# Two joined pair sums a unit, maxima turned in the row scores' ring, inverse sums half a unit later, and an identity in PSUM

## What is computed

```python
xn = _layernorm(x)
# attention: 32 heads of 32 channels, 8 key/value heads
q, k, v = (bitnet_linear(xn, w, s) for w, s in ((q_weight, q_scale), (k_weight, k_scale), (v_weight, v_scale)))
scores = einsum('bhqd,bhkd->bhqk', q, k) / sqrt(32)
attn = softmax(scores)
att = bitnet_linear(einsum('bhqk,bhkd->bhqd', attn, v), o_weight, o_scale)
# FFN: 1024 -> 3584 -> 1024
gate, up = silu(xn @ deq(gate_w)), xn @ deq(up_w)
out = x + att + (gate * up) @ deq(down_w)
```

## Time and profile before

| | us |
|---|---|
| median of 3 runs (lowest, highest) | 2314.91 (2314.68, 2315.96) |
| the profiled execution | 2313.24 |
| its span in the profile | 2311.2 |
| TensorE busy | 2259.1 (98%) |
| VectorE busy | 1808.2 (78%) |
| ScalarE busy | 1591.1 (69%) |
| GpSimd busy | 1036.6 (45%) |

### The profile page before, as it was taken

How to read it: one execution, slowest core, us unless ns; L and a number is a source line. 1 busy time by engine, 2 the same in 40 slices (tenths; PEclk the granted TensorE clock), 3 DMA queues, 4 the chain that set the end, 5 groups by cost and what they waited for, 6 DMA issues and landing times.

```text
span 2311.2 us, 44481 instructions
## 1 busy us (share of the span) xinstructions
PE 2259.1 (98%) x18195; PEld 1015.9 (44%) x18195; DVE 1808.2 (78%) x2305; ACT 1591.1 (69%) x2059; POOL 1036.6 (45%) x598
## 2 busy tenths in 40 slices
PE   6999999999999999999999999999999999999998
PEld 4444344444444444334444444444445444444444
DVE  8878888888888888856677777777777777777777
ACT  6774788888888888852466666666666666666664
POOL 0450689999999999930055553210003222221000
PEclk9999999999999999999999999999999999999999
DMA  5893444444444444433387884131114111114111
GB/s 188 170 205 97 112 92 102 104 94 109 100 107 94 101 106 96 113 97 110 119 107 94 95 97 64 37 119 37 37 64 146 37 37 43 48 39 183 37 37 73
DMA packets 187888, 216.38 MB, mean 94 GB/s; under 512 B 88402, under 2 KB 128210, under 8 KB 186662
## 3 DMA queue, kind: packets, MB, share of 16 engines
q1 hardware_dynamic: 114742, 151.67, 20.8%
q0 software_dynamic: 72944, 61.88, 20.0%
HBM read 164.28 MB, written 69.64 MB: 101 GB/s over the span
## 4 chain that ended last, share of the span: by engine, by line
PE 90%; DVE 5%; ACT 2%; issue 1%; SPq 1%; DMA 1%; DVEq 0%; ACTq 0%; POOL 0%
PE ps L1759 33%; PE ps L1775 17%; PE ps L1523 9%; PE ps L1576 9%; PE ps L1590 9%; PE ps L1728 5%; PE ps L1607 4%; PE ps L1548 3%; DVE zone L1184 1%; DVE sm L1049 1%; ACT zone L869 1%; DVE zone L1088 1%; PE ps L1791 0%; DVE zone L1294 0%; ACT zone L849 0%
## 5 line engine op out<-in xcount | busy, mean ns | idle before, releaser
L1759 PE MATMUL ps<-xT,zone 128*128 128x512 f16 x3584 | 774.2, 379 | 0.0
L1203 DVE TENSOR_REDUCE zone<-ps 128x1 f32<-128x512 f32 x1024 | 636.5, 681 | 102.7 <-PE ps L1523 98.5
L869 ACT ACTIVATE zone<-ps,sm 128x512 f32<-128x512 f32 x1024 | 623.9, 695 | 101.5 <-PE ps L1576 98.4
L690 POOL TENSOR_TENSOR xT<-zone 128x1024 f32<-128x1024 f32 x252 | 617.2, 2675 | 127.0 <-ACT zone L869 127.0
L1440 DVE TENSOR_SCALAR ps<-ps,zone_c 128x1024 f32<-128x1024 f32 x392 | 506.8, 1293 | 162.4 <-PE ps L1759 160.3
L992 ACT ACTIVATE ps<-ps,zone_c 128x1024 f32<-128x1024 f32 x392 | 426.6, 1088 | 248.3 <-PE ps L1759 248.3
L1759 PEld LDWEIGHTS ps<-xT,zone 128*128 128x128 f16 x3584 | 350.6, 98 | 422.5 <-DVE zone L1444 0.3
L1576 PE MATMUL ps<-zone 98*32 98x512 f16 x4096 | 412.9, 381 | 5.9 <-ACT zone L869 4.2
L1523 PE MATMUL ps<-zone 96*32 96x512 f16 (+1 forms) x3946 | 411.2, 380 | 3.6 <-DVE zone L1203 3.6
L1775 PE MATMUL ps<-zone 128*128 128x512 f16 x1792 | 387.1, 379 | 0.0
L1451 DVE TENSOR_SCALAR ps<-ps,zone_c 128x1024 f32<-128x1024 f32 x216 | 279.3, 1293 | 93.0 <-PE ps L1775 92.8
(11 more groups left out here) (141 smaller groups left out, 1438.7 us busy)
## 6 DMA issues: line engine op xcount, KB each, us to landing
zone<-dequantised SPq DMA_DIRECT2D x84, 512.0 KB, 3.7
xT<-xT POOLq DMA_DIRECT2D x31, 1024.0 KB, 8.7
dequantised<-zero_points SPq DMA_DIRECT2D x56, 256.0 KB, 4.0
zone<-zone SPq DMA_DIRECT2D x384, 32.0 KB, 1.9
zone<-_attn_hidden_states_dram SPq DMA_DIRECT2D x16, 512.0 KB, 6.3
zone<-inverse_sums SPq DMA_DIRECT2D x128, 64.0 KB, 2.6
attention<-zone SPq DMA_DIRECT2D x32, 256.0 KB, 2.2
xT<-attention SPq DMA_DIRECT2D x4, 2048.0 KB, 12.1
```

The costliest lines, as they stand in the source:

```text
L690: nc.gpsimd.tensor_tensor(pairs[:, j, hp, :], prob[:, prob_slot(e), :], prob[:, prob_slot(e + 2), :], add).then_inc(s["sum_ok"], 1)
L869: A(prob[:, prob_slot(e), m % 2 * 512:(m % 2 + 1) * 512], ps[:, 3 + m % 3, :], ACT.Exp, scale=gam[:, 0:1]).then_inc(s["exp_ok"], 1)
L1203: V.tensor_reduce(mxs[:, u % 2, half, i % 16:i % 16 + 1], ps[:, (2 * i + half) % 3, :], AX, amax).then_inc(s["max_ok"], 1)
L1759: last = MM(ps[:, 4 * s2 + 2 * m + c, :], ring[:, buf, m * H + g * P:m * H + (g + 1) * P], xT[:, hf, part, g, c * 512:(c + 1) * 512], star ...
```

## The change

`joined_late` holds for units 0 to 29. There `join_late` adds pair sum 2 to pair sum 3 by a second adding DMA, so only j = 1 (k = 2) and j = 3 go through the ones, the latter at k = 12. The maxima are turned into a place of the row scores' ring: `row_place` leaves one out for them in each unit, and the row groups behind them wait accordingly. The steps behind the sums move: `evacuate_sums` to k = 13, `compact_sums` to k = 15, `invert` to k = 6 of the next unit, `store_inverse` to k = 7, `spread_inverse` to k = 13, `head_of` to k = 7, `divide` and `tail_of` to j = 0 and j = 1 of the unit after. `turn_maxima` also turns an identity into PSUM, and `common_maxima` reads it there. In the last turns, ScalarE and GpSimd do two blocks of four in the first two quarters, and stores take two blocks each.

```diff
+def joined_late(u):
+    return u < UNITS - 2
...
-    return 3 * u
+    return 2 * u if u < UNITS - 1 else 2 * u + 1
...
-    return ones_before(u) + (((None, 1, 0, 2) if joined(u) else (0, 1, 2, 3))[j])
+    return ones_before(u) + (((None, 0, None, 1) if joined_late(u) else (None, 1, 0, 2) if joined(u) else (0, 1, 2, 3))[j])
...
+def row_place(c):
+    return c + max(0, (c - 34) // 32)
+def maxima_place(u):
+    return 33 * u + 33 if u else None
...
                     load_v(u // 2 + 1)
-                if k == 7 and u:
+                if k == 7 and u >= 2:
+                    store_inverse(u - 2)
+                if k == (15 if u < UNITS - 1 else 7) and u:
...
                     load_m(u + 1)
-                if k == 5 and u >= 2:
+                if k == 13 and u >= 2:
...
                     load_k(u // 2 + 2)
-                if k == 15 and u:
+                if k == 15 and u == UNITS - 1:
...
-            def store_blocks(n):
-                for b in range(4):
-                    sp.wait_ge(s["turn_ok"], 8 + 4 * n + b + 1)
-                    sp.dma_start(rows_of(out, 1, n)[:, b, :], rows(1, n)[:, b, :]).then_inc(s["out_ok"], 16)
+            def store_turned(n):
+                sp.wait_ge(s["turn_ok"], 8 + 2 * n + 2)
+                sp.dma_start(rows_of(out, 1, n)[:, 0::2, :], rows(1, n)[:, 0::2, :]).then_inc(s["out_ok"], 16)
+            def store_mixed(n):
+                sp.wait_ge(s["mix_ok"], 8 + 2 * n + 2)
+                sp.dma_start(rows_of(out, 1, n)[:, 1::2, :], rows(1, n)[:, 1::2, :]).then_inc(s["out_ok"], 16)
+            def store_pair(n, a):
+                sp.wait_ge(s["turn_ok"], 12 + 4 * (n - 2) + 2 * a + 2)
+                sp.dma_start(rows_of(out, 1, n)[:, 2 * a:2 * a + 2, :], rows(1, n)[:, 2 * a:2 * a + 2, :]).then_inc(s["out_ok"], 16)
...
                 load_block(k)
-            for n in range(4):
-                store_blocks(n)
-            sp.wait_ge(s["out_ok"], 16 * (4 + 16))
+            store_turned(0)
+            store_turned(1)
+            store_pair(2, 0)
+            store_mixed(0)
+            store_pair(2, 1)
+            store_mixed(1)
+            store_pair(3, 0)
+            store_pair(3, 1)
+            sp.wait_ge(s["out_ok"], 16 * (4 + 8))
...
                     pool.wait_ge(s["quad_ok"], 16 * u)
+                elif j == 2 and joined_late(u - 1):
+                    pool.wait_ge(s["late_ok"], 16 * u)
...
+            def join_late(u):
+                pool.wait_ge(s["sum_ok"], duo_of(u, 3, 1) + 1)
+                nc.gpsimd.dma_start(pairs[:, 3, :, :], pairs[:, 2, :, :], accum_op=add, max_dma_last_dim=4096).then_inc(s["late_ok"], 16)
...
                         join_pairs(u)
-                    if u >= 2 and j == 1:
-                        divide(u - 2)
-                    if u >= 2 and j == 3:
-                        tail_of(u - 2)
-            for u in range(UNITS - 2, UNITS):
+                    if j == 3 and joined_late(u):
+                        join_late(u)
+                    if u >= 3 and j == 0:
+                        divide(u - 3)
+                    if u >= 3 and j == 1:
+                        tail_of(u - 3)
+            for u in range(UNITS - 3, UNITS):
...
-            def mix_rows(n):
-                pool.wait_ge(s[f"xr_in{n % 2}"], 16 * (n // 2 + 1))
+            def mix_rows(hf, n):
+                pool.wait_ge(s[f"xr_in{n % 2}"], 16 * (n // 2 + 1) if hf == 0 else 16 * 4)
                 for b in (1, 3):
-                    pool.wait_ge(s["half_ok"], 2 * n + (b + 1) // 2)
-                    nc.gpsimd.tensor_tensor(rows(0, n)[:, b, :], rows(0, n)[:, b, :], turned(n)[:, b // 2, :], add).then_inc(s["mix_ok"], 1)
+                    pool.wait_ge(s["half_ok"], 2 * (4 * hf + n) + (b + 1) // 2)
+                    nc.gpsimd.tensor_tensor(rows(hf, n)[:, b, :], rows(hf, n)[:, b, :], turned(n)[:, b // 2, :], add).then_inc(s["mix_ok"], 1)
...
                         n = 2 * TURNS.index((t + 1) // 2)
-                        mix_rows(n)
-                        mix_rows(n + 1)
+                        mix_rows(0, n)
+                        mix_rows(0, n + 1)
...
                         add_attention(hf, oh, s2)
+            mix_rows(1, 0)
+            mix_rows(1, 1)
...
                     evacuate_values(u - 1)
-                if k == 5 and u:
+                if k == 7 and u >= 3:
+                    head_of(u - 3)
+                if k == (13 if u < UNITS - 1 else 5) and u:
                     evacuate_sums(u - 1)
-                if k == 14 and u >= 2:
-                    head_of(u - 2)
...
                     evacuate_sums(UNITS - 1)
+                elif n == 2:
+                    head_of(UNITS - 3)
...
-            def act_turn(n, s2):
+            def act_turn(hf, n, s2):
                 th = n % 2
+                if hf == 1:
+                    act.wait_ge(s["second_pe"], 2 * HALF_VISITS)
                 for b in (1, 3):
-                    i = 4 * th + b
-                    act.wait_ge(s["turn_pe"], 4 * n + b + 1)
-                    if n >= 2:
-                        act.wait_ge(s["mix_ok"], 2 * (n - 2) + (b + 1) // 2)
+                    i = 8 * hf + 4 * th + b
+                    act.wait_ge(s["turn_pe"], 4 * (4 * hf + n) + b + 1)
+                    if hf or n >= 2:
+                        act.wait_ge(s["mix_ok"], 2 * (4 * hf + n - 2) + (b + 1) // 2)
...
                         for th in range(2):
-                            act_turn(2 * TURNS.index(j) + th, th)
+                            act_turn(0, 2 * TURNS.index(j) + th, th)
...
                             act_down(hf, oh, it, s2)
+            act_turn(1, 0, 0)
+            act_turn(1, 1, 1)
...
                     dve.wait_ge(s["s_pe"], 2 * i + half + 1)
-                    V.tensor_reduce(mxs[:, u % 2, half, i % 16:i % 16 + 1], ps[:, (2 * i + half) % 3, :], AX, amax).then_inc(s["max_ok"], 1)
+                    V.tensor_reduce(mxs[:, u % 2, half, i % 16:i % 16 + 1], ps[:, row_place(2 * i + half) % 3, :], AX, amax).then_inc(s["max_ok"], 1)
...
                 dve.wait_ge(s["m_pe"], u + 1)
-                m = ps[0:16, 7, 0:P]
+                m = ps[0:16, maxima_place(u) % 3 if u else 7, 0:P]
...
                 settle()
-                V.tensor_scalar(diag, id32[0:2 * IT, 0:2 * IT], cmt, None, mult).then_inc(s["dg_ok"], 1)
+                V.tensor_scalar(diag, ps[0:2 * IT, 0, P:P + 2 * IT], cmt, None, mult).then_inc(s["dg_ok"], 1)
...
                     common_maxima()
-                if k == 14 and u:
+                if k == 6 and u >= 2:
+                    invert(u - 2)
+                if k == 14 and u == UNITS - 1:
...
                 dve.wait_ge(s[f"xr_in{n % 2}"], 16 * (n // 2 + 1) if hf == 0 else 16 * 4)
-                for b in range(4) if hf else (0, 2):
+                for b in range(4) if hf == 1 and n >= 2 else (0, 2):
...
                 c = 2 * i + half
-                if c >= 3:
+                if c >= 66 and (c - 34) % 32 == 2:
+                    pe.wait_ge(s["mrow_ok"], (c - 34) // 32 + 1)
+                elif c >= 66 and (c - 34) % 32 < 2:
+                    pe.wait_ge(s["max_ok"], c - 1)
+                elif c >= 3:
...
                     c0 = i % 4 * P + a
-                    last = MM(ps[a:a + wide, c % 3, :], qst[u % 4][0:96, i % 16 // 4, c0:c0 + wide],
+                    last = MM(ps[a:a + wide, row_place(c) % 3, :], qst[u % 4][0:96, i % 16 // 4, c0:c0 + wide],
...
                 pe.wait_ge(s["top_ok"], u + 1)
-                if u >= 2:
-                    pe.wait_ge(s["evd_ok"], u - 1)
-                MM(ps[0:16, 7, 0:P], mtop, id32[:], start=True, stop=True).then_inc(s["m_pe"], 1)
+                if u:
+                    pe.wait_ge(s["max_ok"], 32 * u + 32)
+                MM(ps[0:16, maxima_place(u) % 3 if u else 7, 0:P], mtop, id32[:], start=True, stop=True).then_inc(s["m_pe"], 1)
...
             def pair_sums(u, j):
-                first, last_round = ((2, 3) if joined(u) else (0, 3))
+                first, last_round = (1 if joined_late(u) else 2 if joined(u) else 0), 3
...
                     pe.wait_ge(s["quad_ok"], 16 * (u + 1))
+                if j == 3 and joined_late(u):
+                    pe.wait_ge(s["late_ok"], 16 * (u + 1))
                 if j == first:
-                    pe.wait_ge(s["mrow_ok"], min(u + 2, UNITS))
...
                 pe.wait_ge(s["max_ok"], 2 * STEPS)
+                pe.wait_ge(s["mrow_ok"], UNITS)
...
                 pe.wait_ge(s["cmx_ok"], 1)
+                TR(ps[0:2 * IT, 0, P:P + 2 * IT], id32[0:2 * IT, 0:2 * IT], id32[0:2 * IT, 0:2 * IT])
...
                     values(t // 16, t % 16 // 2 + 1)
-                    if e >= 8:
-                        v, j = (e - 8) // 16, (e - 8) % 16 // 4
-                        if j >= 2 or not joined(v):
-                            pair_sums(v, j)
+                    if 1 <= u < UNITS - 1 and k == 12:
+                        pair_sums(u - 1, 3)
```

(7 more changed lines are left out.)

2 lines of the change are left out of this document (1 added, 1 removed).

## The result

| | before | after |
|---|---|---|
| median (lowest, highest), us | 2314.8 (2313.4, 2316.0), 4 runs | 2340.9 (2328.6, 2348.7), 4 runs |
| the profiled execution; its span | 2313.24; 2311.2 | 2328.62; 2326.8 |

The ratio is 1.0111, interval 1.0092 to 1.0129: slower by 26 us, against a forecast of 7 us faster. Before, the executions agree within 3 us; after, they differ by 20, and the profiled one is the fastest of the four.

A forecast was written before the change was run, and what follows sets the result against it. TensorE's own work was taken as the bound, hardly disturbed. Loop +2, identity product -7 and end -2 sum to -7 us: 2306 for the profiled execution, 2308 for the median, range 2290 to 2315.

The forecast's parts named there:

- the part on the second adding DMA: GpSimd and SyncE in the loop: the second join costs GpSimd 1.11 us a unit, nothing waits, net effect 0.
- the reciprocal: VectorE at step 6, ahead of the maxima: it takes 0.21 us; without it the ring stall would be 0.25, not 0.46.
- Nothing waits: Second adding DMA: lands 8.2 to 10.6 us after issue, is wanted some 14 us later, so no one waits.
- the join on GpSimd: Second adding DMA on GpSimd: costs 1.11 us a unit, raising GpSimd's need from 22.1 to 23.2.
- 0.6 to spare: GpSimd in the loop: with the second join it needs 23.2 us of a 23.86 us unit.
- rival (c): ScalarE's head_of at step 7 waits for GpSimd's divide: 0.5 us a unit, +15, 2323 us; chance 0.13.
- 536 matmuls of sums: TensorE's sum rounds in the profile after: 536 matmuls instead of 776; 30 fewer rounds, 25.8 us off TensorE.
- two stalls: TensorE, per unit: +0.53 without the round at step 0, +0.46 at step 8 from the maxima in the ring.
- the product with the identity: VectorE's product near 974.70 to 984.05: with the identity in PSUM it takes some 0.3 us, saving 7 us.
- the loop: Attention loop: -0.86 - 0.05 + 0.53 + 0.46 = +0.08 us a unit, x 30 = +2 us.
- the end: Last 16 blocks: four go from VectorE to ScalarE and GpSimd, larger last store gives back 0.5; -2 us (0 to -2.7).
- the small product fac: VectorE, after the identity product: sm to sm, it would wait for GpSimd in its turn; identity term then -6 to -7.

The follow-up runs named there:

- small join: The changed kernel, its second adding DMA moving only 128 of 1024 columns of each half: 2314.7 us, ratio 1.0008.
- e9: The kernel before plus a 1 MB copy to scratch memory a unit, issued by GpSimd where the change issues its second join: 2338.2 us, ratio 1.0105.
- e12: The kernel before with the 1 MB copy a unit, and load_m sent by ScalarE at step 9 instead of SyncE at step 8: 2324.2 us, ratio 1.0046.
- e1: The changed kernel, its second adding DMA cut to an eighth of its bytes, with the same instructions and waits: 2314.7 us, ratio 1.0008.
- e4: The kernel before with only the identity in PSUM and the changed last turns: 2305.3 us, ratio 0.9968.

## Why the prediction was wrong

- **The step that failed** is in the part on the second adding DMA: "SyncE issues the same DMAs, its new wait at step 7 (for the reciprocal of step 6) stands ahead of load_m, whose own wait comes later. Nothing in either direction, 0." That its DMAs are the same says nothing of how long their issue takes (8.4 became 11.1 in the median) nor of what has gone out ahead of them. I looked at where the new join lands and who waits for it ("Nothing waits", and nobody does: 8.4 to 10.0), and never at what the new join does to the small loads beside it. The cost is 24 us. The small join and e9 show that the megabyte makes it, and e12 (the same traffic, another queue) that the long units come by way of this load; between the long units the changed kernel and e9 lose nothing. About a third of the long units' excess in the profiled execution is the halved clock behind the waits, for which the forecast had no term either. No rival had any of it, so the range, to 2315, could not hold it. The trace of before had the rows: a load that goes out at up to +1.3 of the join and lands in time, and one that goes out at +1.8 and costs its unit 1.6.
- **A term mis-sized**: the join on GpSimd, 1.11, is 1.56, and GpSimd's need 24.09, not 23.2. It does not have "0.6 to spare" but is the bound once the small loads are in time. Two readings failed. The pair of sums that ends with the join, 5.77 long, began after an idle stretch (633.24 in the earlier trace rows), with nothing ahead of it still running, and I held it against 4.66 out of four sums in a row; the overlap lost at the join was not counted. And the idle time is the 1.18 of its row, not 1.65: 23.78 - 1.18 + 1.56 = 24.16. With it, rival (c), ScalarE waiting for the divide, came true in e1 for 11 us; I had given it 0.13 and 15 us. (About 2 of the 11 fall on unit 30, which is 25.4 there and 23.4 without the join.)
- **Right**: 536 matmuls of sums; the saving of 0.86 a unit eaten by two stalls (0.53 exact; 0.37 for 0.46, and 0.64 less 0.16 is 0.48 by its own terms); the product with the identity, 0.27 and -7.3. Without the join the kernel took 2305.3, where the sum of all terms gave 2306 to 2308. That nearness is partly luck: the loop gave -0.3 instead of +2, and the end nothing instead of -2.
- **Wrong, small**: the end, -2, is 0 to +0.3, since the store of two blocks lands 0.9 to 2 later, not 0.5; the reciprocal, 0.21, is 0.03.
- **A rule carried too far**: by the lock that the Trainium skill describes for two-port instructions (SBUF — State Buffer, "SBUF: two separate sides") I let the small product fac wait for GpSimd in its turn. In e4 it took 0.15 in the middle of four sums of GpSimd. It has one element on each partition; whether that takes it out of the rule, no run here shows. It had no part in the sum.

```profile
977.75 0.15 DVE L1409 TENSOR_SCALAR sm<-sm 128x1 f32<-128x1 f32 x1
...
972.05 9.79 POOL L702 TENSOR_TENSOR xT<-zone 128x1024 f32<-128x1024 f32 x4
```

**What stays open**: why executions of the changed kernel differ by 20 us. The scatter comes with the traffic (e9: 17) and is 5 with small joins. The mean granted clock of the four executions falls from 0.994 to 0.990 as the time rises from 2328.6 to 2348.7; by an estimate from these two numbers, 0.004 of 2330 us, about 9 of the 20 us are the clock behind the waits. Why one execution has more or longer waits than another, no trace shows. In the profiled one, the fastest of the four, TensorE, VectorE, ScalarE and GpSimd wait for one DMA only from 320 to 940 us, `load_m`; the part of that load in the slower ones is inferred. Keeping the adding DMA and shortening SyncE's twelve loads was not tried.

## What to carry to other kernels

A queue's issuing counts as no engine's busy time, so look at it in a timeline before you add traffic: how long before its deadline does each small load that TensorE waits for go out, and what large DMA goes out just ahead of it? Price an instruction put between pipelined ones by the starts of the neighbours on both sides, and then take the engine's whole loop without idling. A new transfer is dangerous less by what waits for it than by what lands behind it.
